# A two-batch attention and feed-forward kernel: the rotation moved to GpSimd, the projection products spread over ten steps, sums and value products paired

## What is computed

```
for each of 2 batches, x of 1024 tokens x 512 channels:
    x = x + 0.5 * ffn(norm(x))          # layer norm, gamma, beta, ternary weights, bias
    n = norm(x)
    q, k, v = n @ w_q.T, n @ w_k.T, n @ w_v.T         # 16 heads of 32
    q, k = rope(q), rope(k)             # x * cos + rot(x) * sin, rot swaps the halves of a head
    p = softmax(q @ k.T * scale)        # causal, in blocks of 64 tokens
    x = x + (p @ v) @ w_o.T
    x = x + 0.5 * ffn(norm(x))
```

## Time and profile before

| | us |
|---|---|
| median of 3 runs (658.33 to 658.71) | 658.5 |
| the profiled execution | 658.63 |
| its span in the trace | 656.8 |
| around the span | 1.8 |
| PE busy | 580.6 |
| DVE busy | 430.4 |
| ACT busy | 298.0 |
| POOL busy | 117.9 |

### The profile page before, as it was taken

How to read it: one execution, slowest core, us unless ns; L and a number is a source line. 1 busy time by engine, 2 the same in 40 slices (tenths; PEclk the granted TensorE clock), 3 DMA queues, 4 the chain that set the end, 5 groups by cost and what they waited for, 6 DMA issues and landing times.

```text
span 656.8 us, 10008 instructions
## 1 busy us (share of the span) xinstructions
PE 580.6 (88%) x3586; PEld 219.9 (33%) x3586; DVE 430.4 (66%) x878; ACT 298.0 (45%) x597; POOL 117.9 (18%) x104
## 2 busy tenths in 40 slices
PE   0574999768789999999999999999999999999876
PEld 0433545333323233233233333233333233333432
DVE  5999747638877677677667767767766762242572
ACT  1722812202135555545645645645655556572320
POOL 1411121202121222213212312322210000000100
PEclk9996999979979999999999999999999999999997
DMA  8811033631312233412212124424310004000011
GB/s 320 325 74 64 1 132 113 201 69 49 96 54 76 66 112 107 137 50 81 73 61 94 54 68 117 165 62 149 112 51 2 1 1 161 33 1 33 33 65 64
DMA packets 43553, 57.95 MB, mean 88 GB/s; under 512 B 3478, under 2 KB 34326, under 8 KB 42480
## 3 DMA queue, kind: packets, MB, share of 16 engines
q1 hardware_dynamic: 42924, 57.21, 26.5%
q10 hardware_dynamic: 580, 0.11, 0.1%
HBM read 32.01 MB, written 25.17 MB: 87 GB/s over the span
## 4 chain that ended last, share of the span: by engine, by line
PE 69%; DVE 21%; issue 3%; ACT 3%; DMA 2%; POOL 1%; SPq 0%; ACTq 0%; DVEq 0%
PE bank L916 12%; PE bank L883 10%; PE bank L1027 10%; PE bank L1017 10%; PE bank L897 8%; PE bank L846 6%; PE bank L836 6%; DVE rot L775 4%; PE bank L954 4%; DVE rmax L758 3%; DVE stats L616 3%; PE bank L826 2%; DVE t L768 2%; DMA rows<-in_L_attn_x_dram 2%; ACT big L509 1%
## 5 line engine op out<-in xcount | busy, mean ns | idle before, releaser
L758 DVE TENSOR_REDUCE rmax<-bank 128x1 f32<-128x512 f32 (+3 forms) x384 | 203.2, 555 | 120.7 <-PE bank L897 115.7
L568 ACT ACTIVATE big<-bank 128x512 f32<-128x512 f32 (+3 forms) x384 | 180.0, 489 | 185.2 <-PE bank L883 182.9
L897 PE MATMUL bank<-kst,qst 104*128 104x512 f16 (+3 forms) x384 | 125.9, 333 | 22.2 <-DVE rmax L758 10.5
L883 PE MATMUL bank<-qst,kst 106*128 106x512 f16 (+3 forms) x384 | 123.4, 332 | 0.7 <-ACT big L568 0.4
L473 POOL TENSOR_TENSOR t<-t,rot 128x512 f32<-128x512 f32 x32 | 41.1, 1284 | 248.5 <-DVE rot L775 248.5
L883 PEld LDWEIGHTS bank<-qst,kst 106*128 106x128 f16 x384 | 36.0, 96 | 141.4 <-ACT big L568 68.9
L1027 PE MATMUL bank<-big,rows 128*32 128x512 f32 (+3 forms) x768 | 81.8, 498 | 0.0
L1017 PE MATMUL bank<-big,ones 128*32 128x512 f32 (+3 forms) x768 | 81.8, 498 | 0.0
L897 PEld LDWEIGHTS bank<-kst,qst 104*128 104x128 f16 x384 | 37.8, 98 | 52.3 <-DVE rmax L758 20.0
L487 POOL TENSOR_TENSOR cl<-cf,ch 128x512 f16<-128x512 f32 x16 | 18.5, 1156 | 155.0 <-ACT ch L598 155.0
L916 PE MATMUL bank<-xh,wh 128*128 128x512 f16 x128 | 39.9, 394 | 6.8 <-DVE xl L652 6.8
(11 more groups left out here) (105 smaller groups left out, 624.3 us busy)
## 6 DMA issues: line engine op xcount, KB each, us to landing
spread<-rhl SPq DMA_DIRECT2D x32, 256.0 KB, 2.2
qst<-spread SPq DMA_DIRECT2D x16, 384.0 KB, 3.7
kst<-spread SPq DMA_DIRECT2D x16, 384.0 KB, 3.9
rows<-in_L_attn_x_dram SPq DMA_DIRECT2D x4, 1024.0 KB, 12.3
x<-rows SPq DMA_DIRECT2D x4, 1024.0 KB, 5.0
spread<-rhl SPq DMA_DIRECT2D x32, 128.0 KB, 2.1
xh<-ch SPq DMA_DIRECT2D x4, 512.0 KB, 3.6
xl<-cl SPq DMA_DIRECT2D x4, 512.0 KB, 5.2
```

The costliest lines, as they stand in the source:

```text
L568: nc.scalar.activation(probs[:, st % P_PLACES, h, 0:n], pb[u % 2][:, 0:n], ACT.Exp, scale=EXP_SCALE).then_inc(s_eb, 1)
L758: nc.vector.tensor_reduce(rmax[:, at:at + 1], pa[u % 3][:, 0:n], AX.X, ALU.max, negate=True).then_inc(s_max, 1)
L883: nc.tensor.matmul(pb[u % 2][:, 0:n], kst[0:ROWS_B, g % SETS, h, j * P:(j + 1) * P], qst[0:ROWS_B, g % SETS, h, q0:q0 + n], start=True, st ...
L897: nc.tensor.matmul(pa[u % 3][:, 0:n], qst[0:ROWS_A, g % SETS, h, i * P:(i + 1) * P], kst[0:ROWS_A, g % SETS, h, half * HALF:half * HALF + ...
```

## The change

1. **Rotation.** ScalarE copies the projection's bank into `t1` in the step behind its last product. GpSimd then does all four of the rotation's instructions from there (two of 64 partitions by sin, one by cos, the sum), with a wait between each and the next. VectorE's three are gone. The rounding, the remainder and both DMAs come 2 to 3 steps later.
2. **Projection.** The 12 products of a tile stand in ten steps (`SLOTS`), one in each, two in the fifth and the tenth. The bank is waited for by `s_copy`.
3. **Pairing.** `PV_LAG` is 9 in place of 7. So the sums of a key step and the value products of the key step before fall into one step, every fourth, directly behind each other.
4. **Transposes of the maxima** take a turn in the three banks of A (`a_bank`, `max_bank`) between the fifth and the sixth unit of the next head; two A products beside it wait for a maximum one product nearer, and one for ScalarE's copy.
5. **Starts and lags.** `A_START` 6 to 11, `B_START` 18 to 20; the reciprocal three steps earlier against the last value product, scaling and splitting one step earlier; `Y3_STEP` and `F3_STEP` of batch 0's first half 15 steps later; both DMAs of columns and context 4 steps later.

```diff
-A_START, B_START = 6, 18
-SUM_LAG, PV_LAG = 5, 7
+A_START, B_START = 11, 20
+SUM_LAG, PV_LAG = 5, 9
 P_PLACES = 4
+
+SLOTS = [(0,), (1,), (2,), (3,), (4, 5), (6,), (7,), (8,), (9,), (10, 11)]
+MAX_PLACE = 5
...
+        def a_bank(u):
+
+            return pa[(u + max(0, (u - MAX_PLACE) // A_UNITS)) % 3]
+
+        def max_bank(n):
+
+            return pa[(A_UNITS * (n + 1) + MAX_PLACE + n) % 3]
...
-        Y3_STEP = [O0_START + 55 + 2 * n for n in range(4)] + [O0_START + 97 + 2 * n for n in range(4)]
-        F3_STEP = [O0_START + 65 + 4 * r for r in range(4)] + [O0_START + 107 + 4 * r for r in range(4)]
+        Y3_STEP = [O0_START + 70 + 2 * n for n in range(4)] + [O0_START + 97 + 2 * n for n in range(4)]
+        F3_STEP = [O0_START + 80 + 4 * r for r in range(4)] + [O0_START + 107 + 4 * r for r in range(4)]
...
-                if u := proj_after(k, 8):
+                if u := proj_after(k, 11):
                     g, m = u
                     n = 4 * g + m
                     sp.wait_ge(s_rl, n + 1)
...
-                if u := proj_after(k, 11):
+                if u := proj_after(k, 14):
...
-                if u := proj_after(k, 3):
+                if u := proj_after(k, 2):
                     n = 4 * u[0] + u[1]
-                    pool.wait_ge(s_rot, n + 1)
+                    cols = slice(u[1] // 2 * HALF, (u[1] // 2 + 1) * HALF)
+                    pool.wait_ge(s_copy, n + 1)
...
+                    for first in (0, P // 2):
+                        other = P // 2 - first
+                        pool.tensor_tensor(rot[first:first + P // 2, n % 2, :], t1[other:other + P // 2, n % 2, :],
+                                           sin_s[other:other + P // 2, cols], ALU.mult).then_inc(s_rot, 1)
+                        pool.wait_ge(s_rot, 3 * n + (2 if first else 1))
+                    pool.tensor_tensor(t1[:, n % 2, :], t1[:, n % 2, :], cos_s[:, cols], ALU.mult).then_inc(s_rot, 1)
+                    pool.wait_ge(s_rot, 3 * n + 3)
                     pool.tensor_tensor(t1[:, n % 2, :], t1[:, n % 2, :], rot[:, n % 2, :], ALU.add).then_inc(s_rope, 1)
-                if u := proj_after(k, 7):
+                if u := proj_after(k, 9):
...
+                if u := proj_after(k, 1):
+                    n = 4 * u[0] + u[1]
+                    act.wait_ge(s_proj, n + 1)
+                    if n >= 2:
+                        act.wait_ge(s_rl, n - 1)
+                    nc.scalar.activation(t1[:, n % 2, :], pp[:, :], ACT.Copy).then_inc(s_copy, 1)
...
-                if u := proj_after(k, 6):
+                if u := proj_after(k, 8):
                     n = 4 * u[0] + u[1]
                     act.wait_ge(s_rope, n + 1)
...
-                if c := ctx_half(k, 0):
+                if c := ctx_half(k, -3):
                     n = 2 * c[0] + c[1]
                     act.wait_ge(s_sum, 12 * c[0] + 4 + 8 * c[1])
...
-                if c := ctx_half(k, 2):
+                if c := ctx_half(k, 1):
                     n = 2 * c[0] + c[1]
                     dve.wait_ge(s_rec, n + 1)
...
+                if e := max_head(k, MAX_PLACE + 1):
+                    n = GH * e[0] + e[1]
+                    pe.wait_ge(s_max, A_UNITS * (n + 1) + (MAX_PLACE - 2 if n + 1 < GH * ALL else 0))
+                    pe.wait_ge(s_mp, n + 1)
+                    nc.tensor.transpose(max_bank(n)[0:2 * TILES, 0:P // 2].bitcast(F16),
...
-                    if u >= 3:
+                    heads, turn = divmod(u - MAX_PLACE, A_UNITS)
+                    if heads > 0 and turn == 2:
+                        pe.wait_ge(s_mrows, heads)
+                    elif heads > 0 and turn < 2:
+                        pe.wait_ge(s_max, u - 1)
+                    elif u >= 3:
                         pe.wait_ge(s_max, u - 2)
```

More of the change, by code:

```diff
@@ L463, in _ @@
             rstd_of(0, 1, 6)
+            roots = 6
+            lows = 0
             for k in range(LAST_STEP):
@@ L869, in _ @@
             evacuated = 0
-            moved = 0
             for k in range(LAST_STEP):
@@ L908, in _ @@
                         if evacuated:
[L909 to L911 removed]
+                            pe.wait_ge(s_copy, evacuated)
                     og = g % GROUPS
[L913 removed]
+                    for n in SLOTS[i]:
                         a, cc = divmod(n, CC)
```

76 lines of the change are left out of this document (28 added, 48 removed).

## The result

The changed kernel takes 649.56 us (median of 4 runs, 647.92 to 650.09) against 658.61 (658.33 to 658.71) before: a ratio of 0.986, 95% interval 0.985 to 0.987. That is 9.1 us less. The forecast was 655, 3.9 less in the profiled execution: the sign and the range held, the size did not.

What follows compares the result with a forecast made beforehand. In the long middle, what TensorE issues and how it is held up sets the pace. Terms -18.2 - 14.4 + 21.8 + 9.8 - 4.1 + 1.2 = -3.9 took 658.6 to 654.7, said as 655 us; range 638 to 671.

Steps and rivals of the forecast that it cites:

- the old waits: TensorE's waits for maxima behind VectorE's rotation (10.5 us) and of the maxima's transposes (3.9) go: -14.4 us.
- the switches: Entering and leaving the 32-wide shape for sums and value products: about 96 of 192 visits saved, 0.19 each, -18.2 us.
- the start: Before B's start: the rotation's chain lets the fifth A unit and B begin earlier, -4.1 us.
- The new waits: B waits for exponentials in four-step windows between pairs, most behind the reciprocal: +21.8 us to step 384, +9.8 after.
- The end: Last value products come two steps later, behind feed-forward products that covered the chain to the output products: +1.2 us.
- The copy and the rotation's chain: ScalarE's 0.60 us copies hide beside visits; GpSimd's rotation, 5.3 us with gaps, is hidden in the middle: nothing.
- the exponentials keeping up: Rival: ScalarE keeps up; 623 us without any new wait, 639 with half, taken for this case; chance 0.25.
- copies in front: Rival: ScalarE's copies stand in front of the exponentials, up to 0.6 us per head with a projection: 672 us; chance 0.13.
- slow rotation: Rival: from 7.7 us of rotation on, ScalarE's rounding blocks the exponentials: 687 us; chance 0.05.
- a pair that saves nothing: Rival: a pair's second group starts as if it came from outside the 32-wide shape: 673 us; chance 0.07.

Runs made afterwards that it cites:

- the split pair: Changed kernel with the value products in the same step but directly behind B, no longer directly behind the sums: 670.1 us, ratio 1.018.
- the unpaired changed kernel: Changed kernel with value products at lag 7 in place of 9, reciprocal, scaling and splitting keeping their steps: 659.3 us, ratio 1.001.

## Why the forecast held in sign and not in size

The mechanism was right and the terms were mis-sized. The term most wrong is the old waits, put at 14.4 us where 21.0 were to be had; next come the switches (18.2 for 22.0), and against both the start (4.1 for 0.9).

**The switches** were mis-sized, in the cautious direction. I took 0.19 a visit between 0 and 0.24; 94 visits fewer between B's start and its end gave 22.0 us, 0.23 each, and the split pair lost 20.5 in time. The 0.14 that I read behind a visit was exit (0.12) and 0.03 inside. The Trainium skill (TensorEngine Tiling (Array Packing), Key Properties) says that a change of the tiling mode drains TensorE, and a change of tile alone does not. The trace agrees: from the sums to the value products it loses nothing beyond the 0.03 us inside any visit.

**The old waits** were the larger miss. The view of waits gave 10.5 + 3.9 us; by the distance of starts the same waits, with the few of B, were 21.0. The view counts idle time from the modelled end of a matmul, which lies after its last column. The earlier trace rows had it in them: the row at 189.96 says 0.39, yet the A product ahead of it started at 189.30 and streams 256 columns, 0.11 us, so 0.55 were lost. Some 58 waits at about 0.11 each would be those 6.6 us. That these waits go with the rotation is shown by the unpaired changed kernel, where A and the transposes wait 1.0 us.

**The new waits** were forecast at 31.6; 30.4 are there, though that counts what is left of A's: in the five groups up to 431.1 15.7 us (11.0 of B, 4.5 of A), 3.1 a group where I had 3.9, and from there to B's end 14.7. The mechanism was right row by row: in a steady group the windows without projection cost 1.2 us (0.36, 0.20, 0.36 and 0.31; 1.5 forecast), and the fourth B of the second half 1.14 (1.2). The wait of the first half's reciprocal, 0.6, did not occur. The last stretch was right in size and also takes work moved there: 43 feed-forward products became 48 and 16 transposes 32, so that its 59.6 us hold 3.4 us more of columns.

**The start** failed: -4.1 forecast, -0.9 measured. The step that failed is the moment from which the rotation's chain was counted. ScalarE's copy of the first tile is queued behind its work on the columns, and the projection waits for it:

```profile
79.78 0.68 ACT L599 ACTIVATE t<-bank 128x512 f32<-128x512 f32 x1
...
80.55 3.11 POOL L499 TENSOR_TENSOR rot<-t,sin_s 64x512 f32<-64x512 f32 x2 [20.51 <-ACT t L599]
80.61 0.38 PE L944 MATMUL bank<-xh,wh 128*128 128x512 f16 x1 [2.40 <-ACT t L599]
```

That was a wait the change adds, for which I had named no queue: 2.4 us. TensorE arrived at the fifth A unit at 135.8, not 131.9, and the rotation of the first group's last tile ended at 130.5, not 126.9. Rotation, rounding and remainder then took what I had said. From the remainder's end to the fifth unit it was 9.3 us for 8.3, with the mask rows' transfers ahead of the spread's, so the unit came at 141.7, not 137.1. (The sum for the second group, 137.1 with 30 steps at 0.846 and 1.5, gives 164.0, not the 164.6 written there; that is 0.6 of the error the other way.)

**The end** gave back 2.0 us for 1.2: the idle time was as worked out, the low clock behind it was not in the sum. Other executions of the same end took 53.0 and 54.9 us, so the 0.8 may be chance.

**The copy and the rotation's chain**, taken as hidden, were hidden. ScalarE's rounding waited for the sum 8 times, 19.6 us in all, each time before 176 us; from B's start on, four instructions of 1.27 us a tile cost nothing. VectorE's relief took A's and the transposes' waits away, and with the new order of the projection it is worth 0.9 us a steady group; in the total the move of work into the last group takes most of it back. *Of the rivals*, the exponentials keeping up came nearest (639 with half of the waits); copies in front, slow rotation and a pair that saves nothing are excluded by the time and by the split pair.

Put together: old waits -6.6, switches -3.8, new waits -1.2, moved work and other gaps +2.1, start +3.2, end +0.8 are -5.5 us, the distance from -3.9 to -9.4.

## What to carry to other kernels

Put products that use the same part-array shape directly behind each other even if the gaps they leave elsewhere then wait: adjacency was worth 21 us, the longer windows cost 10 to 16 of them, and moving one activation pair by a step gave 4.7 back. Measure a wait of TensorE by the distance of two starts less the columns between them, not by the idle time in the list of waits, which lost a third here. Before calling a gain that of an edit, look where in the profile it lies: with the mask rows moved, 3.1 of the 4.0 us lay in a stretch that the edit does not touch. When an operation that empties a bank moves, ask first when the bank comes free and what stands ahead in the queue of the engine that frees it, also in the start-up.

## What the hardware showed that I had not expected

**VectorE is held by GpSimd in some instructions only.** In the changed kernel an `mparts` instruction over 8 columns took 1.11 to 1.13 us where it fell beside one of GpSimd's, and ended 0.02 to 0.03 us after it (301.62 to 302.74, GpSimd's L502 from 301.44 to 302.71); without overlap it takes 0.17. With the rotation on VectorE it was the `TENSOR_SCALAR` of the packing (0.99 us mean) that fell beside GpSimd's single sum, and it was held in the same way. Maxima from PSUM and products with one input in PSUM were not. GpSimd is held in turn: the first two products by sin took 3.11 us for 2.6 beside VectorE's remainder. The Trainium skill (SBUF — State Buffer, Who interferes with whom) calls this an exclusive lock on a shared pair of ports, taken by a VectorE instruction with two SBUF inputs, beside a GpSimd instruction that reads SBUF, or in a two-port mode; in that mode, it says, whoever comes second is blocked for the other's whole instruction. Durations, ends and exceptions here agree with it. I had looked for this price in GpSimd's durations only, not in VectorE's.

**A stall of TensorE can have a second price.** With the rotation back on VectorE, behind ten waits of 2.1 to 2.6 us for the bank eight sum products took 1.86 to 1.94 us in place of 1.07, and behind one of 2.28 us they did not; behind the 2.9 us at the end the clock fell in one execution and not in another.
